# Four graph layers on one core: GpSimd waits for each pair's gathers to land in passes 3 and 4

## The chip, the core and the metric

The kernel runs on one core of one Trainium2 chip. The core has five engines that run on their own and meet at semaphores: TensorE (PE in the rows, its weight loads PEld), VectorE (DVE), ScalarE (ACT), GpSimd (POOL) and SyncE (SP). SP, ACT and POOL start transfers, and all transfers share 16 DMA engines. The metric is device time in microseconds: 3856.42 us, the median of three runs of the kernel before (3853.22 to 3861.42).

## The reference

Four message-passing layers over the same graph of 6250 nodes and 106250 edges, each added to x and followed by a layer normalisation. Cut to its core:

```python
edge_index = jnp.stack([src, dst])
x = _layernorm(x + _L0(x, edge_index, edge_attr, ...))   # MLP on [x[src], edge_attr], mean over dst
x = _layernorm(x + _L1(x, src, dst, ...))                # sum of scaled x[src], batch norm
x = _layernorm(x + _L2(x, src, dst, ...))                # mean of x[src], elu
x = _layernorm(x + _L3(x, edge_index, edge_type, edge_weight, ...))

def _rgcn_conv(x, src, dst, edge_type, edge_weight, W, root, bias):   # twice in _L3
    xj = x[src]
    m = sum over r of (edge_type == r)[:, None] * (xj @ W[r])
    m = m * edge_weight[:, None]
    return segment_sum(m, dst) + x @ root + bias
```

The edges are sorted by dst. The change is in the two convolutions of the last layer.

## The kernel before, in words

The edges are cut into 832 tiles of 128, four tiles to a group (208 groups), two groups to a pair (104 pairs). Pass 0 does layer 0, passes 1 and 2 do layers 1 and 2, and passes 3 and 4 are the two convolutions of layer 3. Each pass ends in per-node work that is woven into the pass as blocks of nodes become complete.

Passes 3 and 4 read a table in device memory, table_rel, that holds x @ W[r] for every node and each of the four relations, one row of 512 bytes each. For most pairs GpSimd fetches the eight tiles of rows: `fetch` (L649, the DMA at L652) issues one indirect DMA per tile, 128 rows of 512 bytes, by the indices in `reli`. The eight land in one of four buffers `late_gat`, and each adds 16 to that buffer's semaphore `late_gathered`. `late_pool` (L719) does so pair after pair; from the fifth pair on it waits first for `late_seg`, the count of pairs that PE has finished, since the buffer is free only then. Nothing else stands in GpSimd's queue in these passes.

ScalarE builds the weighted one-hot tiles of a pair (`late_act`, L2650; L2660 and L2665), after a wait on `late_seg` for their own four buffers. PE (`late_pe`, L1615) waits for the landed gathers, for those one-hots and for the sum's bank, and multiplies the eight tiles into the segment sum (the 16 matmuls of L1654), which raises `late_seg`. VectorE adds the sum into `acc` (L1483).

Ten pairs of a pass (h = 10, 20, ..., 100), and in pass 4 five more (h = 21, 41, ...), are not gathered: PE builds their sums as dense counts times the node matrix. That work is spread over the pairs between, in pieces: `unit_fill` and `extra_fill` (L1670, L1683; matmuls L1679, L1690), copies to SBUF by VectorE (L1489, L1582), `extra_use` and `unit_use` (L1694, L1704; L1700, L1715), and L1645 at the pair itself. In pass 3 SP stores each built piece (880 KB) in `kept`, and in pass 4 loads it again. So 94 pairs are gathered in pass 3 and 89 in pass 4, 183 in all, with 1462 gathers (one tile of padding in each pass is left out).

The wait of PE on the gathers, which the change repeats on GpSimd:

```python
pe.wait_ge(late_gathered[n % LATE], (n // LATE + 1) * 16 * PU - late_padded(n) * 16)
```

`LATE` is 4 (buffers), `PU` is 8 (tiles of a pair), n counts the gathered pairs through both passes. `gate` is a semaphore that nothing waits for.

Of the kernel before, what the change touches and what calls it, by code (L numbers as in the profile page):

```python
# [69 lines left out]
PU = 2 * U  # L70
# [8 lines left out]
LATE, LATE_HOTS, LATE_BANKS, LATE_LAG, NODE_LAG = 4, 4, 2, 2, 5  # L79
# [50 lines left out]
def gnn(nc, x_rows, x_cols, src, dst, first, etype, eweight, ea_cols, W1a, b1a, b2b, biases, weights, out):  # L130
    with ExitStack() as ctx:
# [3 lines left out]
        def sem(name):  # L135
            return ctx.enter_context(nc.semaphore(name))

        def sems(name, n):
            return [sem(f"{name}{i}") for i in range(n)]
# [199 lines left out]
        gate = sem("gate")  # L339
# [16 lines left out]
        late_gathered = sems("late_gathered", LATE)  # L356
# [292 lines left out]
        def fetch(pool, p, g, into, landed, skipped=0):  # L649
            for u in range(U - skipped):  # L650
                t = g * U + u
                pool.indirect_dma_start(into[:, u, :], None, tables[p],  # L652
                                        bass.IndirectOffsetOnAxis(ap=idx_of(p)[:, t:t + 1].bitcast(U32), axis=0)
                                        ).then_inc(landed, 16)
# [27 lines left out]
        def padded(g):  # L682
            return PADDED if g == GROUPS - 1 else 0


        def slow_pool(pool, p, before):
            if p == 3:
                pool.wait_ge(s_sources, 2)
                pool.sem_inc(gate, 1)
            def stored():  # L690
                for s, n in zip(table_stored[p], STORED[p]):
                    pool.wait_ge(s, n)
                    pool.sem_inc(gate, 1)

            with pool.If(before > 0):
                stored()
                with pool.Fori(0, before) as r:
                    for g in range(GROUPS):
                        pool.wait_ge(slow_seg, (before * (p - 1) + r) * GROUPS + (g + 1))
                        pool.sem_inc(gate, 1)  # L700
                        fetch(pool, p, g, gat[g % RING], gathered[g % RING])
            pool.wait_ge(slow_seg, before * (p * GROUPS) + RING)
            pool.sem_inc(gate, 1)
            stored()
# [14 lines left out]
        def late_pool(pool, p, before):  # L719
            slow_pool(pool, p, before)  # L720
            for i, h in enumerate(L_PAIRS[p - 3]):
                n = (p - 3) * len(G_PAIRS) + i
                if n >= LATE:
                    pool.wait_ge(late_seg, seg_of(n - LATE))
                    pool.sem_inc(gate, 1)
                for o in range(2):
                    fetch(pool, p, 2 * h + o, late_gat[n % LATE][:, o * U:(o + 1) * U, :], late_gathered[n % LATE],
                          padded(2 * h + o))


        def late_padded(n):
            lasts = (len(G_PAIRS) - 1, len(G_PAIRS) + len(L_PAIRS[1]) - 1)
            return sum(PADDED for m in lasts if m <= n and m % LATE == n % LATE)

        def seg_of(n):
            p = int(n >= len(G_PAIRS))
            return p * PAIRS + L_PAIRS[p][n - p * len(G_PAIRS)] + 1
# [2074 lines left out]
        @block.gpsimd  # L2812
        def _(pool):
            start_pool(pool)
            before = load_rounds(pool)
            pass0_pool(pool, before)
            node0_pool(pool)
            for p in (1, 2):
                wide_pool(pool, p, before)
            for p in (3, 4):  # L2820
                late_pool(pool, p, before)
# [84 lines left out]
```

## Time and profile before

| what | value |
|---|---|
| median of three runs | 3856.42 us |
| span of the profiled execution | 4761.8 us |
| PE busy | 3833.3 us (81%) |
| POOL busy | 2652.2 us (56%) |
| DVE busy | 2287.6 us (48%) |
| ACT busy | 2017.5 us (42%) |
| gathers of passes 3 and 4 (L652, table_rel) | 1462, 1385.7 us busy |
| DMA queue of GpSimd (q0) | 235.32 MB, 18.7% of 16 engines |

Only the span is given for the profiled execution; it is 905.4 us longer than the median of the runs. Shares are of the span. POOL counts as busy while it makes the descriptors of a gather; the transfer itself comes after that. "issue" is time in which an engine waited for nothing that the profile shows, and "remote" or "another core or an unknown queue" is a wait whose releaser it cannot name.

### The profile page before, as it was taken

The numbers are of one execution on the slowest core, as the hardware profiler recorded it, in microseconds if no ns is written. First come the engines' busy times: TensorE is split into PE (matmuls) and PEld (weight loads), VectorE is DVE, ScalarE is ACT, GpSimd is POOL, SyncE is SP. The second block draws the span as 40 slices with busy tenths as digits, with TensorE's granted clock in tenths as the row PEclk, the third lists the DMA queues.
The fourth block names the chain that finished last, engine by engine and source line by source line (L and its number), as shares of the span: only waits on it lengthen the run. The fifth ranks groups of instructions, "written<-read, shape, count | busy, mean of one in ns | idle before, by whom it ended". The sixth has DMA issues, their size and how long they took to land.

```text
span 4761.8 us, 69331 instructions
## 1 busy us (share of the span) xinstructions
PE 3833.3 (81%) x23096; PEld 3228.5 (68%) x23096; DVE 2287.6 (48%) x7830; ACT 2017.5 (42%) x4824; POOL 2652.2 (56%) x2744
## 2 busy tenths in 40 slices
PE   5888888888888997899577778777766777777777
PEld 4777777777776886788466666555555666766666
DVE  5777777777676555666434334333321222222222
ACT  3444434444445554565444444444443333433332
POOL 5666666566542654555565565555656556564554
PEclk7999998998899998999788888888887788888878
DMA  6555555555555664666234333333333334443333
GB/s 197 151 147 149 152 149 150 148 148 149 144 151 145 149 152 105 160 172 165 89 127 137 128 134 131 125 116 127 127 114 105 118 113 124 128 125 112 121 115 97
DMA packets 438618, 642.39 MB, mean 135 GB/s; under 512 B 266274, under 2 KB 310818, under 8 KB 438115
## 3 DMA queue, kind: packets, MB, share of 16 engines
q1 hardware_dynamic: 310162, 375.66, 25.2%
q0 software_dynamic: 100880, 235.32, 18.7%
q10 hardware_dynamic: 27202, 26.78, 1.8%
q8 instruction: 191, 3.13, 0.3%
q14 instruction: 183, 1.50, 0.1%
HBM read 468.80 MB, written 168.73 MB: 134 GB/s over the span
## 4 chain that ended last, share of the span: by engine, by line
PE 28%; another core or an unknown queue 10%; issue 8%; DVE 5%; ACT 1%; DVEq 0%; DMA 0%; POOL 0%; ACTq 0%; POOLq 0%; SPq 0%
PE bank L1715 9%; PE bank L1654 6%; PE bank L1679 4%; PE bank L1700 3%; PE bank L1690 3%; PE bank L1645 1%; DVE w_both L1489 1%; DVE work L1557 1%; DVE work L1489 1%; DVE late_lo L1537 1%; PE bank L2353 0%; PE bank L2370 0%; DVE work L1582 0%; ACT work L2665 0%
## 5 line engine op out<-in xcount | busy, mean ns | idle before, releaser
L652 POOL DMA_INDIRECT work<-table_rel,reli x1462 | 1385.7, 948 | 1060.0 <-issue 426.4
L652 POOL DMA_INDIRECT work<-table_pre,srci x831 | 816.7, 983 | 537.6 <-issue 237.3
L2660 ACT ACTIVATE work<-iota,local 128x72 f32<-128x72 f32 x1464 | 378.4, 344 | 609.1 <-remote 346.8
L1034 ACT ACTIVATE X<-bank 128x468 uint8<-128x468 f32 (+1 forms) x624 | 323.9, 545 | 708.7 <-PE bank L976 375.1
L1654 PE MATMUL bank<-work 128*128 128x72 f32 x2928 | 425.0, 290 | 245.9 <-issue 234.8
L1654 PEld LDWEIGHTS bank<-work 128*128 128x128 f32 x2928 | 417.4, 212 | 265.5 <-issue 242.5
L2665 ACT ACTIVATE work<-work,ew,src_both 128x72 f32<-128x72 f32 x1464 | 515.4, 436 | 15.7 <-remote 9.7
L937 PE MATMUL bank<-w_both,work 128*128 128x256 f32 x1664 | 473.2, 409 | 33.3 <-issue 14.5
L1406 PE MATMUL bank<-counts,piece_hi 128*128 128x468 f32 x1176 | 464.7, 395 | 28.4 <-issue 12.9
L1406 PE MATMUL bank<-counts,piece_lo 128*128 128x468 f32 x1176 | 450.2, 383 | 0.0
L949 PE MATMUL bank<-work 128*128 128x64 f32 x3328 | 423.0, 281 | 22.3 <-issue 21.4
L949 PEld LDWEIGHTS bank<-work 128*128 128x128 f32 x3328 | 417.6, 201 | 29.5 <-issue 25.0
L976 PE MATMUL bank<-X 128*128 128x234 bf16 (+3 forms) x2080 | 293.6, 269 | 158.9 <-ACT X L1034 107.9
L1582 DVE COPY work<-bank 128x440 f32<-128x440 f32 x200 | 118.5, 614 | 560.6 <-remote 307.4
L937 PEld LDWEIGHTS bank<-w_both,work 128*128 128x128 f32 x1664 | 310.8, 205 | 71.5 <-issue 31.3
L871 DVE TENSOR_TENSOR work<-work,bank 128x512 f32<-128x512 f32 x416 | 274.0, 682 | 169.5 <-PE bank L937 99.5
L976 PEld LDWEIGHTS bank<-X 128*128 128x128 bf16 x2080 | 184.4, 104 | 244.8 <-issue 169.9
L1679 PE MATMUL bank<-work,late_lo 128*128 128x440 bf16 x1050 | 260.1, 382 | 109.8 <-DVE work L1489 36.7
L825 DVE TENSOR_SCALAR X<-X 128x600 bf16<-128x600 f16 (+1 forms) x624 | 234.5, 439 | 230.8 <-PE bank L976 176.5
L652 POOL DMA_INDIRECT work<-table_mean,srci x207 | 208.7, 1008 | 175.8 <-PE bank L1392 88.5
L1489 DVE COPY w_both<-bank 128x440 f32<-128x440 f32 x200 | 118.2, 613 | 349.8 <-remote 223.4
L652 POOL DMA_INDIRECT work<-table_gcn,srci x207 | 206.5, 998 | 139.7 <-issue 63.5
(326 smaller groups left out, 6489.9 us busy)
## 6 DMA issues: line engine op xcount, KB each, us to landing
work<-ea_cols SPq DMA_DIRECT2D x208, 256.0 KB
kept<-work SPq DMA_DIRECT2D x50, 880.0 KB
kept<-w_both SPq DMA_DIRECT2D x50, 880.0 KB
work<-kept SPq DMA_DIRECT2D x50, 880.0 KB
w_both<-kept SPq DMA_DIRECT2D x50, 880.0 KB
adj<-X SPq DMA_DIRECT2D x156, 225.0 KB
work<-adj SPq DMA_DIRECT2D x60, 585.0 KB
work<-table_rel,reli POOLq DMA_INDIRECT x1462
```

The source lines that it names most:

```text
L652: pool.indirect_dma_start(into[:, u, :], None, tables[p], bass.IndirectOffsetOnAxis(ap=idx_of(p)[:, t:t + 1].bitcast(U32), axis=0)).then_i ...
L871: dve.tensor_tensor(g, g, bank[q % 2 * 2 + h][:, :], ALU.add).then_inc(pre_added, 1)
L937: mm = pe.matmul(bank[q % 2 * 2 + h][:, j * HID:(j + 1) * HID], ea[:, slot, u * P:(u + 1) * P], w1a[:, 1, :], start=True, stop=True)
L949: pe.matmul(into[:, c * WIN:(c + 1) * WIN], gat0[:, q % SLOTS0, u, c * F:(c + 1) * F], hot0[:, hq, u, 0:WIN], start=(u == 0), stop=(u == U ...
L976: mm = pe.matmul(into[:, :, A_OFF[u]:A_OFF[u] + w], hot_lo[q % HOTS][:, u, :], code[:, j % A_CODES, at:at + (hi - lo) * w].rearrange("p (h ...
L1034: act.activation(stage[:, j % A_STAGES, lo * AW:hi * AW], bank[A_BANKS_AT[b % 2]][:, 0:(hi - lo) * AW], ACT.Copy).then_inc(a_taken, 1)
L1406: mm = pe.matmul(bank[D_BANKS[step % 2]][:, 0:D * AW], x[:, i * CT + t, :], counts[n % 2][:, t, :], start=(i * CT + t == BLANK and x is pi ...
L1654: mm = pe.matmul(bank[4 + m % LATE_BANKS][:, 0:PAIR_WIN], late_gat[n % LATE][:, u, :], late_hot[:, n % LATE_HOTS, u * PAIR_WIN:(u + 1) * P ...
L1679: mm = pe.matmul(bank[A_BANKS_AT[u % 2]][:, 0:RHI * CW], late_lo[:, n // RANGES % 2, u * PIECES + i, :], late_code[n % 2 * U + u], start=( ...
L1715: mm = pe.matmul(bank[D_BANK][:, 0:U * CW].rearrange("p (u c) -> p u c", u=U), rows[:, at, :], late_a[n % 2][:, :, t, :], start=(at == BLA ...
L2660: ins = act.activation(hot3[:, u, :], iota[:, 0:PAIR_WIN], ACT.Abs, bias=local[:, t:t + 1], scale=-1.0)
L2665: ins = act.activation(hot3[:, u, :], hot3[:, u, :], ACT.Relu, bias=ew[:, t:t + 1], scale=src_lo[:, t:t + 1])
```

## The change

Behind the gathers of each pair GpSimd waits until the semaphore of that pair's buffer shows that all of them have landed, and raises `gate` by one. The count is written as a function of the pair's number.

```diff
                 for o in range(2):
                     fetch(pool, p, 2 * h + o, late_gat[n % LATE][:, o * U:(o + 1) * U, :], late_gathered[n % LATE],
                           padded(2 * h + o))
+                pool.wait_ge(late_gathered[n % LATE], late_landed(n, PU - padded(2 * h + 1)))
+                pool.sem_inc(gate, 1)
+
+        def late_landed(n, tiles):
+            before = late_padded(n - LATE) if n >= LATE else 0
+            return (n // LATE * PU + tiles - before) * 16
```

On POOL at the start of pass 3 there stood, in the kernel before (a row's waits are those that stand ahead of its first instruction):

```order
L702 ISA
L652 DMA work<-table_rel,reli 128x128 [waits slow_seg,table3_stored0,table3_stored1]
L652 DMA work<-table_rel,reli 128x128 x31
L652 DMA work<-table_rel,reli 128x128 [waits late_seg]
L652 DMA work<-table_rel,reli 128x128 x7
L652 DMA work<-table_rel,reli 128x128 [waits late_seg]
```

And at the same place in the changed kernel, with the four buffers' semaphores told apart by their numbers:

```order
L702 ISA
L652 DMA work<-table_rel,reli 128x128 [waits slow_seg,table3_stored0,table3_stored1]
L652 DMA work<-table_rel,reli 128x128 x7
L652 DMA work<-table_rel,reli 128x128 [waits late_gathered0]
L652 DMA work<-table_rel,reli 128x128 x7
L652 DMA work<-table_rel,reli 128x128 [waits late_gathered1]
L652 DMA work<-table_rel,reli 128x128 x7
L652 DMA work<-table_rel,reli 128x128 [waits late_gathered2]
L652 DMA work<-table_rel,reli 128x128 x7
L652 DMA work<-table_rel,reli 128x128 [waits late_gathered3,late_seg]
```

No gather changes its place; the first 32, which stood in one run, now stand in four, and each later pair has a second wait ahead of it. The other engines' orders are the same.

## Rows read from the trace of the kernel before

**Rows 1.** Busy time by stage: window, its length, engines (instructions), granted clock, DMA, GB/s.
```profile
core 0: us, PE busy (x) PEld busy (x) DVE busy (x) ACT busy (x) POOL busy (x), PEclk, DMA share, GB/s
0.00:1440.00 1440.00, 1203.36 (x8698) 1035.16 (x8699) 1012.28 (x4051) 585.70 (x1130) 836.93 (x857) 0.92 0.54 154
1440.00:1810.00 370.00, 346.18 (x1816) 297.27 (x1814) 210.58 (x582) 191.11 (x266) 181.15 (x183) 0.98 0.60 144
1810.00:1890.00 80.00, 67.89 (x346) 58.45 (x344) 43.24 (x117) 38.07 (x49) 34.19 (x35) 0.88 0.44 107
1890.00:2290.00 400.00, 365.15 (x1825) 308.29 (x1825) 254.67 (x721) 232.17 (x260) 214.24 (x208) 0.95 0.59 155
2290.00:2335.00 45.00, 21.45 (x79) 10.60 (x77) 29.77 (x104) 28.08 (x74) 15.00 (x16) 0.77 0.26 90
2335.00:3517.00 1182.00, 897.34 (x4999) 707.62 (x4999) 434.53 (x1253) 496.21 (x1583) 697.43 (x736) 0.84 0.38 127
3517.00:3560.00 43.00, 24.18 (x106) 18.69 (x107) 10.61 (x40) 26.09 (x80) 11.38 (x13) 0.69 0.25 85
3560.00:4762.00 1202.00, 907.77 (x5236) 792.46 (x5235) 291.95 (x966) 420.03 (x1385) 661.93 (x699) 0.81 0.38 115
```

**Rows 2.** Chain of waits by line: 2320 to 3535 us, then 3535 to 4762 us.
```profile
by line: another core or an unknown queue 25.5%; PE bank L1679 16.2%; PE bank L1715 13.8%; issue 13.4%; PE bank L1654 8.4%; DVE w_both L1489 3.1%; DVE work L1557 2.9%; DVE work L1489 2.7%; DVE late_lo L1537 2.5%; PE bank L1645 1.7%; PE bank
...
by line: PE bank L1715 22.7%; issue 18.6%; PE bank L1654 13.3%; PE bank L1700 13.1%; another core or an unknown queue 12.4%; PE bank L1690 11.3%; PE bank L1645 2.1%; DVE work L1582 1.3%; PE bank L2757 0.6%; DVE late_lo L1546 0.6%; DVE work 
```

**Rows 3.** Chain in order of time, from 3573 us: start, length, what.
```profile
3573.72 0.28 PE bank L1654
3574.00 2.52 issue
3576.52 0.28 PE bank L1654
```

**Rows 4.** Groups of instructions on POOL: line, count | busy, mean ns | idle before, releasers.
```profile
L652 POOL DMA_INDIRECT work<-table_rel,reli x1462 | 1385.7, 948 | 1060.0 <-issue 426.4 <-PE bank L1654 359.0 <-remote 215.7
```

**Rows 5.** Instructions in order of time, 4107 to 4114 us: start, length, engine, [idle before].
```profile
4107.97 1.90 PE L1654 MATMUL bank<-work 128*128 128x72 f32 x16
...
4108.94 0.95 POOL L652 DMA_INDIRECT work<-table_rel,reli  x1 [0.30 <-issue]
4110.19 0.95 POOL L652 DMA_INDIRECT work<-table_rel,reli  x1 [0.31 <-issue]
...
4112.80 2.07 ACT L2660 ACTIVATE work<-iota,local 128x72 f32<-128x72 f32 x8 [7.19 <-remote]
...
4113.55 0.94 POOL L652 DMA_INDIRECT work<-table_rel,reli  x1 [2.40 <-remote]
```

**Rows 6.** Busy time in half microseconds behind a gather that ends at 3827.47 us.
```profile
3827.50:3828.00 0.50, 0.00 (x0) 0.00 (x0) 0.00 (x0) 0.00 (x0) 0.00 (x0) 0.50 0.00 0
3828.00:3828.50 0.50, 0.00 (x0) 0.00 (x0) 0.00 (x0) 0.00 (x0) 0.00 (x0) 0.50 0.51 123
3828.50:3829.00 0.50, 0.00 (x0) 0.00 (x0) 0.00 (x0) 0.00 (x0) 0.00 (x0) 0.50 0.03 8
```

**Rows 7.** That gather in order of time, and the wait beyond it.
```profile
3826.53 0.94 POOL L652 DMA_INDIRECT work<-table_rel,reli  x1 [0.30 <-issue]
3829.81 0.34 DVE L1588 COPY w_both<-bank 128x176 f32<-128x176 f32 x1 [18.26 <-remote]
```

**Rows 8.** Chain in order of time at the start of pass 4.
```profile
3540.67 3.39 DMA table_rel<-work
3544.20 0.77 issue
3544.96 0.95 POOL work L652
...
3553.73 3.26 DMA work<-table_rel,reli
3557.03 3.69 PE bank L1654 x16
```

## The prediction

> **What bounds the kernel now.** I read the busy time by stage first [rows 1]. Pass 0 ends near 1440 us, passes 1 and 2 fill 1440 to 2290 us, and the two passes that change are the stages of 1182 and 1202 us, with a start of 45 and of 43 us ahead of them. The reader is to see that PE is nearly full in passes 1 and 2 (346 of 370 us, 365 of 400 us) and is not in passes 3 and 4 (897 of 1182 and 908 of 1202 us, at granted clocks of 0.84 and 0.81).
>
> The chain of waits says what fills the rest [rows 2]. In pass 3, 25.5% of 1215 us (310 us) is a wait whose releaser the profile cannot name and 13.4% (163 us) is "issue", in which the engine waited for nothing. In pass 4 they are 12.4% (152 us) and 18.6% (228 us) of 1227 us. Together 853 us. Looked at closely, the "issue" is odd: PE runs one matmul of 0.28 us and then stands for 2.52 us, again and again, with its operands there and no wait [rows 3]. The profiled span is 4761.8 us and the median of the runs 3856.4 us, so 905 us of this execution are not in the timed runs. Since 853 us of strange standing lie in just these two passes, I take it that most of it belongs to the profiling, and that the timed passes 3 and 4 are much shorter than 1182 and 1202 us.
>
> How short can they be? The other stages, with PE's busy time taken to the full clock, need at least 1203.36 x 0.92 = 1107 us (pass 0), 346.18 x 0.98 = 339 us and 365.15 x 0.95 = 347 us (passes 1 and 2), and with the three starts of 80, 45 and 43 us as they stand that is 1961 us [rows 1]. That leaves passes 3 and 4 at most 3856 - 1961 = 1895 us. PE's own work there at the full clock is 897.34 x 0.84 + 907.77 x 0.81 = 1489 us. GpSimd's is more: 1462 gathers with 1385.7 us busy, 0.948 us each [rows 4], and 0.30 us from the end of one to the start of the next, with nothing to wait for [rows 5], so 1385.7 + 1462 x 0.30 = 1824 us. By these rows GpSimd fills 1824 of at most 1895 us and is the bound of both passes in the timed runs. In the profiled execution it isn't: there it stands 359.0 us for L1654 and 215.7 us for unnamed releasers, because PE has not given its buffers back [rows 4].
>
> **The change, part by part.** 183 waits and as many `sem_inc` are added; nothing is removed, and no gather changes its place. Behind the wait on POOL's queue stand the next pair's eight gathers and nothing else; PE waits for those. The last wait of a pass hides under the start of pass 4 (28 us without a gather, since table_rel is still being stored) or has nothing behind it, so 181 count.
>
> The price of one wait: the time from the end of a gather's descriptors to its landing, plus the time from a semaphore to the next gather's start, less the 0.30 us that would have passed anyway. The restart is 0.77 us: the store of table_rel lands at 3544.20 and the first gather starts at 3544.96 us [rows 8]. For the landing no wait of POOL stands in the trace, so I bound it. Below: behind the gather that ends at 3827.47 us nothing else moves, 0.51 of the DMA engines' time is busy in the half microsecond to 3828.50 and 0.03 in the next [rows 6, 7], so its bytes are in between 1.03 and 1.53 us after its end. Above: the last gather of pass 4's first pair starts at 3553.73, ends its 0.95 us at 3554.68, and PE starts on it at 3557.03 us, 2.35 us later [rows 8], with two loads of 880 KB started just before. I take 1.4 us, the upper half of the quiet case, since it is quiet behind most gathers (DMA share 0.38 in both stages [rows 1]) and the semaphore comes behind the bytes.
>
> Price of one: 1.4 + 0.77 - 0.30 = 1.87 us, bounds 1.50 and 2.82 us. Of 181: 338 us, bounds 272 and 510 us. A restart that a full ring of buffers costs already isn't paid twice; I let that go, since where GpSimd is the bound its buffers are free before it comes to them.
>
> The Trainium skill ("DMA: Bandwidth & Descriptors", section "Anatomy of one DMA — SWDGE (gpsimd) path") fits about 2.0 us plus the bytes over 436 GB/s to a DMA issued from GpSimd, most of it the receipt of the last write. For 64 KB that is 2.15 us from the start, so by an estimate from that page 1.20 us behind the 0.948 us, a price of 1.67 us and a sum of 302 us; the trace, with its bytes still arriving 1.03 to 1.53 us after the end [rows 6, 7], agrees, rather on the later side.
>
> Of the 338 us some fits into what GpSimd has spare, 0 to 71 us (1895 - 1824); I take half, 35 us. After the change GpSimd needs 1824 + 338 = 2162 us for what took at most 1895, and no other engine comes near: PE 1489 us at the full clock. Sum: 3856 + 338 - 35 = 4159 us; bounds 3856 + 272 - 71 = 4057 and 3856 + 510 = 4366 us. The sum is made for the timed runs. Against the profiled span it could not be made: there the 575 us that GpSimd already stands for its buffers [rows 4] would take in all 338 us.
>
> **The rivals.**
>
> Faster, because the pauses free what the gathers hold up. At 4107.97 us PE runs a pair's 16 matmuls, done by 4109.87; ScalarE's next one-hots, which wait for that count, start at 4112.80 and GpSimd's next gather at 4113.55 us, and both only after the running gathers had ended at 4111.14 us [rows 5]. VectorE stands 18.26 us until 2.3 us after the last gather of a burst [rows 7]. So PE's increments arrive when GpSimd has gone quiet, and a pause behind every pair would let them in sooner. If that holds in timed runs too, bursts halved save half of the unnamed waits, 231 of 462 us. But GpSimd would still need its time, so this decides only where a gather costs less than in these rows: the pass must hold the added 338 us, which it does under (1895 - 338) / 1462 = 1.065 us a gather. At 0.948 us GpSimd needs 1386 + 338 = 1724 us against 1895 - 231 = 1664 us, so the gain is 1895 - 1724 = 171 us and the time 3685 us. Against it: the 0.30 us between gathers is the same in quiet and in crowded stretches, and the 853 us fit the 905 us that the timed runs do not have.
>
> Nothing, because GpSimd is not the bound in the timed runs. If the 0.30 us were the profiling's, the gathers would take 1386 us, leave 509 us, and hide all 338: 3856 us. Halfway, at 1.10 us a gather, they take 1608 us, with the waits 1946, 51 us over 1895: 3907 us.
>
> Dearer: a landing that meets the 880 KB stores and loads of `kept` more often than not, at the upper price, or PE's clock falling further as it waits more. By the upper price 4366 us.
>
> That the wait never stops GpSimd is excluded: a gather's bytes arrive over 1 us after its descriptors [rows 6], and the pair's last gather is what the wait is for.
>
> **How the numbers follow.** The forecast, 4057 to 4320 us, has a chance of 0.57. Partly hidden, 3864 to 4057 us: 0.16. Nothing, which means within 0.2% (about 8 us, what a measurement of this kernel can tell): 0.07. Faster: 0.13. Above 4320 us: 0.07. Slower is 0.57 + 0.16 + 0.07 = 0.80. The range for 8 in 10 leaves out the faster case and the dearest one, 0.20 together: 3850 to 4320 us. The likeliest time is 4159 us.
>
> **What would show it.** In the profile of the changed kernel each pair's first gather should stand 1.5 to 2.8 us, with the landing of table_rel's rows as the releaser, some 181 times, and the stands for L1654 should shrink. No burst should be longer than eight gathers, and the unnamed waits of DVE and ACT should fall below about 12 us each. The profiled span may even shrink while the timed runs grow, which would bear out that the holding belongs to the profiling. A timed run under 3864 us would say that a gather costs less than 1.065 us in timed runs, or that the increments are held there too; one near 4159 us, that GpSimd was the bound.

## The result, and the profile after

| | before | after |
|---|---|---|
| median of 4 runs in turn, us | 3855.5 (3853.22 to 3861.42) | 4358.97 (4353.01 to 4363.55) |
| ratio | | 1.1301 (1.1285 to 1.1317) |
| span of the profiled execution, us | 4761.8 in the first profile, 3861.5 in a second | 4354.7 |

The change costs 503 us, 13.0%. The forecast was 4159 us in a range of 3850 to 4320 us: the sign, the bound and the way it works were right, the time lies 200 us above the likeliest and 39 us above the range.

The profile ahead of the prediction turned out to be that of a disturbed execution (its span of 4761.8 us against a median of 3856), so a second one of the unchanged kernel was taken (before_again, below), and all of the rows after are set beside that. One run of wait_every2 below, 4983.87 us at a granted clock of 0.649 where its others had 0.92, is left out of its median. First before_again's busy time by stage, in the columns of [rows 1]; the last three rows are pass 3, the start of pass 4, and pass 4.

```profile
core 0: us, PE busy (x) PEld busy (x) DVE busy (x) ACT busy (x) POOL busy (x), PEclk, DMA share, GB/s
0.00:1965.00 1965.00, 1861.48 (x12642) 1635.54 (x12642) 1510.39 (x5454) 1068.63 (x1699) 1277.37 (x1280) 0.98 0.63 175
...
2000.00:2915.00 915.00, 820.85 (x5005) 664.28 (x5006) 442.00 (x1289) 506.41 (x1615) 692.41 (x731) 0.94 0.49 165
2915.00:2960.00 45.00, 29.61 (x127) 21.94 (x126) 10.48 (x40) 16.86 (x52) 20.37 (x22) 0.69 0.28 86
2960.00:3861.00 901.00, 804.45 (x5248) 745.10 (x5248) 291.95 (x966) 432.29 (x1427) 671.87 (x710) 0.91 0.49 155
```

The same view of the changed kernel:

```profile
0.00:1965.00 1965.00, 1862.83 (x12636) 1635.21 (x12637) 1508.86 (x5448) 1068.91 (x1697) 1273.51 (x1279) 0.98 0.63 175
...
2000.00:3160.00 1160.00, 930.79 (x5000) 732.89 (x5000) 444.38 (x1297) 508.44 (x1621) 688.16 (x728) 0.85 0.39 130
3160.00:3200.00 40.00, 25.92 (x113) 21.48 (x113) 2.99 (x14) 7.99 (x23) 21.71 (x23) 0.63 0.20 53
3200.00:4355.00 1155.00, 891.59 (x5267) 821.92 (x5266) 297.35 (x992) 441.18 (x1454) 672.29 (x711) 0.83 0.40 123
```

Passes 0 to 2 agree to a few microseconds: the first gather of pass 3 starts at 1998.24 us before and at 1999.87 us after. All of the 493 us between the two profiled executions lies in passes 3 and 4: 245 us in the one, 254 us in the other, and 5 us less in the start between. GpSimd's busy time is the same in both and fills only three fifths of its stage after, where it filled three quarters before. PE is busy for longer at a lower granted clock (0.85 for 0.94, 0.83 for 0.91); brought to the full clock it works 1531 us after and 1504 us before, so it has no more to do, it is only held back.

The chain of waits by line, from 2000 us to the end, first before_again, then the changed kernel, says by whom:

```profile
by line: POOL work L652 64.7%; issue 21.4%; DMA work<-table_rel,reli 4.9%; PE bank L1654 3.8%; PE bank L1715 1.8%; PE bank L1700 1.0%; PE bank L1690 0.5%; PE bank L1645 0.5%; PE bank L1679 0.3%; DMA table_rel<-work 0.2%; PE bank L2353 0.1%;
```

```profile
by line: POOL work L652 50.5%; issue 23.6%; DMA work<-table_rel,reli 22.9%; PE bank L1660 0.8%; PE bank L1721 0.4%; PE bank L1685 0.4%; PE bank L1651 0.2%; PE bank L2376 0.1%; PE bank L2359 0.1%; DMA table_rel<-work 0.1%; POOLq L730 0.1%; P
```

Already before, 86% of the end is set by GpSimd's gathers and the "issue" between them; the unnamed releasers of [rows 2] are gone without any change of the kernel. After, the landing of gathers takes 22.9% of 2354 us, 539 us, where it had 4.9% of 1861 us, 91 us. (L1654 has become L1660, and other lines behind the change have moved by six.)

GpSimd's gathers as a group, the answer to [rows 4], in before_again and then after (line, count, busy and mean ns, idle before and its releasers):

```profile
L652 POOL DMA_INDIRECT work<-table_rel,reli x1462 | 1386.1, 948 | 494.6 <-issue 439.1 <-DMA table_rel<-work 49.4 <-PE bank L1654 6.1
```

```profile
L652 POOL DMA_INDIRECT work<-table_rel,reli x1462 | 1382.3, 945 | 989.7 <-DMA work<-table_rel,reli 509.5
```

A gather costs the same 0.945 to 0.948 us. The idle time before gathers doubles, by 495.1 us, and that is the whole of the loss. The waits of POOL after 2000 us split it (us in total, times, longest):

```profile
POOL work L652 <- DMA work<-table_rel,reli: 509.5, 176, 6.3
POOL work L652 <- issue: 422.3, 1281, 5.4
POOL work L652 <- DMA table_rel<-work: 48.0, 2, 30.5
POOL work L652 <- PE bank L1651: 9.9, 3, 3.9
```

The 176 stands for a landing have a mean of 2.89 us. Instruction by instruction, five more are put down to something else: two among "issue" (5.38 and 3.97 us) and the three for L1651. With them it is 181 stands, as the prediction counted, 528.8 us in all, 2.92 us each. A gap of 0.30 us would have been there anyway: 181 x 2.62 = 474 us. Beyond that, 16 of the "issue" gaps are longer than 0.30 us, by 23 us together (see the last section). 474 + 23, less 4 us of busy time, are the 493 us between the two executions. The stands differ: 107 of the 181 last 2.3 to 2.6 us, 74 are longer, 20 of these over 4 us.

One stand in order of time (start, length, engine, [idle before]), with no large transfer beside it:

```profile
2071.55 0.95 POOL L652 DMA_INDIRECT work<-table_rel,reli  x1 [0.30 <-issue]
2074.10 1.24 PE L1660 MATMUL bank<-work 128*128 128x72 f32 x7 [3.77 <-DMA work<-table_rel,reli]
2074.93 0.94 POOL L652 DMA_INDIRECT work<-table_rel,reli  x1 [2.43 <-DMA work<-table_rel,reli]
```

and the chain through it (start, length, what):

```profile
2071.55 2.51 DMA work<-table_rel,reli
2074.06 0.02 issue
2074.08 0.02 POOLq L730
2074.10 0.08 issue
2074.18 0.02 POOLq L725
2074.19 0.73 issue
2074.93 0.94 POOL work L652
```

The gather's landing is told at 2074.06 us, 1.56 us after its 0.95 us; the new wait (L730) and the old one for the buffer (L725) pass through the sequencer, and the next gather starts 0.87 us after the landing. Where SP has put a store of 880 KB on its way meanwhile, the same stand looks like this:

```profile
2262.46 0.94 POOL L652 DMA_INDIRECT work<-table_rel,reli  x1 [0.30 <-issue]
...
2262.81 0.32 SPq L2422 DMA_DIRECT2D kept<-work  x1
...
2268.85 3.33 PE L1660 MATMUL bank<-work 128*128 128x72 f32 x16 [2.68 <-DMA work<-table_rel,reli]
2269.68 0.94 POOL L652 DMA_INDIRECT work<-table_rel,reli  x1 [6.28 <-DMA work<-table_rel,reli]
```

The landing now comes 6.35 us after the gather's start (2268.81), not 2.51. PE stands 2.68 us for the same landing.

### The profile page after: what moved, and what is told of

It is laid out like the page before. It is cut to its first block, busy times and chain, and to the rows that moved or that the text cites. A ratio compares the mean times of both kernels' runs of the same rounds, so it can differ in the third digit from the quotient of the medians.

```text
span 4354.7 us, 69514 instructions
## 1 busy us (share of the span) xinstructions
PE 3732.0 (86%) x23096; PEld 3223.4 (74%) x23096; DVE 2276.1 (52%) x7830; ACT 2043.7 (47%) x4824; POOL 2658.9 (61%) x2744
## 4 chain that ended last, share of the span: by engine, by line
POOL 27%; issue 13%; DMA 13%; PE 1%; ACT 0%; POOLq 0%; DVE 0%; ACTq 0%; DVEq 0%; SPq 0%
POOL work L652 27%; DMA work<-table_rel,reli 12%; PE bank L1660 0%; PE bank L1721 0%; PE bank L1685 0%; PE bank L2359 0%; DMA table_rel<-work 0%; PE bank L1651 0%; PE bank L2376 0%; POOLq L730 0%; POOLq L725 0%; PE bank L2357 0%; DVE X L2589 0%; PE bank L2456 0%; ACT L2500 0%
## 5 line engine op out<-in xcount | busy, mean ns | idle before, releaser
L1660 PE MATMUL bank<-work 128*128 128x72 f32 x2928 | 505.7, 345 | 483.9 <-DMA work<-table_rel,reli 483.7
L1660 PEld LDWEIGHTS bank<-work 128*128 128x128 f32 x2928 | 481.1, 256 | 542.1 <-DMA work<-table_rel,reli 539.4
L943 PE MATMUL bank<-w_both,work 128*128 128x256 f32 x1664 | 432.5, 385 | 18.2 <-DVE work L877 9.4
L955 PE MATMUL bank<-work 128*128 128x64 f32 x3328 | 399.2, 273 | 5.5 <-DVE hist L824 4.8
L955 PEld LDWEIGHTS bank<-work 128*128 128x128 f32 x3328 | 393.3, 193 | 12.5 <-issue 9.4
L1047 ACT ACTIVATE work<-work 128x512 f32<-128x512 f32 x416 | 254.0, 629 | 213.2 <-DVE work L877 212.0
L943 PEld LDWEIGHTS bank<-w_both,work 128*128 128x128 f32 x1664 | 289.6, 192 | 44.2 <-issue 9.8
L1588 DVE COPY work<-bank 128x440 f32<-128x440 f32 x200 | 115.8, 614 | 388.7 <-PE bank L1696 386.2
L1495 DVE COPY work<-bank 128x440 f32<-128x440 f32 x200 | 116.7, 612 | 315.9 <-PE bank L1685 315.8
L982 PE MATMUL bank<-X 128*128 128x234 bf16 (+3 forms) x2080 | 261.4, 251 | 14.2 <-ACT X L1040 13.7
```

Of the source, the lines that this page charges most:

```text
L943: mm = pe.matmul(bank[q % 2 * 2 + h][:, j * HID:(j + 1) * HID], ea[:, slot, u * P:(u + 1) * P], w1a[:, 1, :], start=True, stop=True)
L955: pe.matmul(into[:, c * WIN:(c + 1) * WIN], gat0[:, q % SLOTS0, u, c * F:(c + 1) * F], hot0[:, hq, u, 0:WIN], start=(u == 0), stop=(u == U ...
L982: mm = pe.matmul(into[:, :, A_OFF[u]:A_OFF[u] + w], hot_lo[q % HOTS][:, u, :], code[:, j % A_CODES, at:at + (hi - lo) * w].rearrange("p (h ...
L1047: act.activation(pairs, pairs, ACT.Relu).then_inc(done, 1)
L1660: mm = pe.matmul(bank[4 + m % LATE_BANKS][:, 0:PAIR_WIN], late_gat[n % LATE][:, u, :], late_hot[:, n % LATE_HOTS, u * PAIR_WIN:(u + 1) * P ...
```

## The experiments

Eleven runs follow, the first of the kernel before itself. The question came in two parts: is it the wait itself, the landing behind it, or something that the first profile showed (increments held up)? And why 2.62 us and not 1.87? Ratios, and the differences in us, are to the kernel before as timed in turn with each: median 3854.4 us for before_again, wait_prev, wait_every2 and wait_after1, 3859.88 us for seven, after_nokept, before_nokept and six_built, 3855.81 us for wait_after2, after1_nokept and after2_nokept.

**before_again**, no edit.

> The kernel before, unchanged, for a second profile. Theory A (GpSimd's gathers bound passes 3 and 4 of the kernel before): if this execution is profiled without the 905 us that the first one had on top, passes 0 to 2 end near 1965 us as in the changed kernel, passes 3 and 4 take some 1890 us, and GpSimd stands there little but its 0.30 us between gathers (under 60 us for anything else). Theory B (GpSimd is not the bound, the engines wait for each other's counts): GpSimd stands 300 us or more for L1654. Time by both: 3856 us.

3863.34 us in the one profiled execution, span 3861.5 us. From the first gather of pass 3 (1998.24 us) to the last of pass 4 (3846.92 us) GpSimd goes from gather to gather:

```profile
2508.22 0.95 POOL L652 DMA_INDIRECT work<-table_rel,reli  x1 [0.30 <-issue]
2509.47 0.94 POOL L652 DMA_INDIRECT work<-table_rel,reli  x1 [0.30 <-issue]
2510.72 0.95 POOL L652 DMA_INDIRECT work<-table_rel,reli  x1 [0.30 <-issue]
```

Of 1462 gathers none stands for over 0.6 us but the first of each pass; the stands for L1654 are 6.1 us, not 359. So GpSimd is the bound without reserve, and the held increments of [rows 5 to 7] aren't there to be released.

**seven**: seven of a pair's eight tiles are gathered, with no wait; PE waits for as many.

```diff
-                          padded(2 * h + o))
+                          o)
...
-                    pe.wait_ge(late_gathered[n % LATE], (n // LATE + 1) * 16 * PU - late_padded(n) * 16)
+                    pe.wait_ge(late_gathered[n % LATE], (n // LATE + 1) * 16 * (PU - 1))
```

> The kernel before, without any wait, but GpSimd gathers seven of a pair's eight tiles and PE multiplies what was left in the eighth place (that part of the sums is left out), so 181 gathers fewer. Theory A (GpSimd is the bound of passes 3 and 4): 181 x (0.948 + 0.305) = 227 us less, 3629 us, or some 30 us more where PE comes to be the bound in places. Theory B (GpSimd merely keeps step with PE): no change, over 3830 us.

3636.21 us, 0.9415 (0.9400 to 0.9429): 224 us (3859.88 to 3636.21) for 181 gathers fewer, which at 0.948 + 0.30 us are 226 us. Almost every microsecond taken from GpSimd comes off the end, so nearly every one put on it must be paid.

**wait_prev**: the wait stands where the change has it, but for the pair before.

```diff
+                if i:
+                    last = PU - padded(2 * L_PAIRS[p - 3][i - 1] + 1)
+                    pool.wait_ge(late_gathered[(n - 1) % LATE], late_landed(n - 1, last))
+                    pool.sem_inc(gate, 1)
```

> GpSimd waits behind each pair not for this pair's gathers but for those of the pair before, so as many waits and as many raises of gate as in the changed kernel, each for something that was issued 10 us earlier. Theory A (the price is the time to land, with nothing issued meanwhile): 3856 to 3875 us. Theory B (the waits themselves, or fewer gathers in flight, cost the time): near 4359 us, or at least half of the 503 us, over 4100.

3858.07 us, 1.0004 (0.9995 to 1.0014). Its waits of POOL:

```profile
POOL work L652 <- issue: 432.8, 1418, 0.6
...
POOL work L652 <- DMA work<-table_rel,reli: 13.4, 44, 0.3
```

The same instructions, a wait and an increment behind every pair, cost nothing: no gap grows past 0.6 us. What costs is only that the eight gathers just issued haven't landed.

**wait_every2**: the change's wait behind every second pair.

```diff
-                pool.wait_ge(late_gathered[n % LATE], late_landed(n, PU - padded(2 * h + 1)))
-                pool.sem_inc(gate, 1)
+                if i % 2:
+                    pool.wait_ge(late_gathered[n % LATE], late_landed(n, PU - padded(2 * h + 1)))
+                    pool.sem_inc(gate, 1)
```

> The wait stands behind every second pair only, for that pair's gathers. Theory A: half of the waits, half of the price: 3856 + 503 / 2 = 4108 us, between 4080 and 4130. Theory B (the buffers: a pause leaves PE without a pair in hand, which two pairs in a row would heal): under 3950 us.

4135.15 us, the median of three runs (4129.63 to 4145.44), 1.0737 (1.0706 to 1.0768): 281 us, 5 us above the range expected and somewhat more than half of the 503. POOL's view has 258.5 us in 85 stands, 3.04 us each. With the five that it puts down to something else they are 90 stands, 250 us beyond the 0.30, 2.78 us each for the 2.62 of the changed kernel. The waits add up one by one, with no slack that the first ones would use up; all 14 of the gaps of 1.86 us (last section) are there too, not half of them.

**wait_after1** and **wait_after2**: the wait for a pair stands behind the first, or the second, gather of the next.

```diff
-                for o in range(2):
-                    fetch(pool, p, 2 * h + o, late_gat[n % LATE][:, o * U:(o + 1) * U, :], late_gathered[n % LATE],
-                          padded(2 * h + o))
-                pool.wait_ge(late_gathered[n % LATE], late_landed(n, PU - padded(2 * h + 1)))
-                pool.sem_inc(gate, 1)
+                for u in range(PU - padded(2 * h + 1)):
+                    if u == 1 and i:    # wait_after2: u == 2
+                        last = PU - padded(2 * L_PAIRS[p - 3][i - 1] + 1)
+                        pool.wait_ge(late_gathered[(n - 1) % LATE], late_landed(n - 1, last))
+                        pool.sem_inc(gate, 1)
+                    t = h * PU + u
+                    pool.indirect_dma_start(late_gat[n % LATE][:, u, :], None, tables[p],
+                                            bass.IndirectOffsetOnAxis(ap=idx_of(p)[:, t:t + 1].bitcast(U32), axis=0)
+                                            ).then_inc(late_gathered[n % LATE], 16)
```

> The same wait for a pair's gathers, but put behind the first gather of the next pair, so 1.25 us of issuing lie beside the landing. In the changed kernel GpSimd stood 509.5 us in 176 waits, 2.90 us each, of which 0.30 would have passed anyway. Theory A: each wait gets 1.25 us cheaper, 2.60 - 1.25 = 1.35 us, 181 x 1.35 = 244 us more than the kernel before: 4100 us, between 4070 and 4130. Theory B (a fixed price for each wait): still near 4359 us.

> The wait behind the second gather of the next pair, so 2.50 us of issuing lie beside the landing, with the 880 KB transfers as they are. Theory A: the quiet waits (2.43 us) cost nothing more and only those beside transfers do; in the last such kernel 60 stood 3.64 us, here 3.64 - 1.25 - 0.30 = 2.1 us each, 125 us: 3980 us. Theory C (the transfers' delay is a fixed span, which the second gather hides too): 55 x (3.95 - 2.50 - 0.30) = 63 us, 3920 us or less.

wait_after1: 4197.35 us, 1.088 (1.0858 to 1.0903), 343 us lost where I had expected 244. wait_after2: 3957.79 us, 1.0261 (1.0242 to 1.0280), 102 us, between the 125 of theory A and the 63 of theory C. Their waits for landings, in this order:

```profile
POOL work L732 <- DMA work<-table_rel,reli: 331.2, 165, 5.1
```

```profile
POOL work L732 <- DMA work<-table_rel,reli: 111.6, 90, 3.6
```

(In wait_after1, 18 more gaps, 70.8 us, stand under "issue".) A gather takes 1.25 us of GpSimd's time, so one issued ahead should hide 1.25 us of a stand, 181 x 1.25 = 226 us. The first hid 160 (503 to 343), the second 241.

**after_nokept** and **before_nokept**: the 880 KB stores and loads of `kept` are cut to 16 columns, in the changed kernel and in the one before.

```diff
-                    sp.dma_start(kept[k:k + 1, :, :].rearrange("o p c -> p (o c)"), late_a[k % 2].rearrange("p u t c -> p (u t c)")
+                    sp.dma_start(kept[k:k + 1, :, :].rearrange("o p c -> p (o c)")[:, 0:16], late_a[k % 2].rearrange("p u t c -> p (u t c)")[:, 0:16]
...
-                sp.dma_start(late_a[k % 2].rearrange("p u t c -> p (u t c)"), kept[k:k + 1, :, :].rearrange("o p c -> p (o c)")
+                sp.dma_start(late_a[k % 2].rearrange("p u t c -> p (u t c)")[:, 0:16], kept[k:k + 1, :, :].rearrange("o p c -> p (o c)")[:, 0:16]
```

> The changed kernel, but SP stores and loads only 16 of the 1760 columns of each built piece, so that the 200 transfers of 880 KB are gone from passes 3 and 4 (the rest of the pieces is left as it stood, that part of the sums is wrong). Theory A1 (the landing takes longer where these transfers run beside it): the quiet stand of 2.43 us remains, 181 x (2.43 - 0.30) = 385 us over the kernel before, 4240 us. Theory A2 (the stand is a fixed latency, the long ones have another cause): 4340 to 4365 us.

> The kernel before with the same transfers cut to 16 of 1760 columns. Theory A (GpSimd's issuing bounds it): within 10 us of 3856 us. Theory B (DMA traffic bounds it): at least 50 us less.

after_nokept: 4274.8 us, 1.1066 (1.1049 to 1.1082), 415 us over before. before_nokept: 3859.38 us, 0.9997 (0.9988 to 1.0006), so without the waits these transfers cost nothing. The stands of after_nokept:

```profile
POOL work L652 <- DMA work<-table_rel,reli: 433.9, 175, 4.0
```

2.48 us each for 2.89, and 13 of the 181 longer than 2.6 us for 74: the transfers explain some 88 of the 503 us (503 less 415). The rest is the bare landing and restart, 181 x 2.18 = 394 us, and 22 us in the 14 gaps of 1.86 us of the last section; the 385 us expected had neither these gaps nor a quiet stand above 2.43 us.

**after1_nokept** and **after2_nokept**: wait_after1 and wait_after2 with the same cut of `kept` (the edits are those two together).

> The wait behind the first gather of the next pair, with the 880 KB transfers of the built pieces cut to 16 of 1760 columns (that part of the sums is wrong). With those transfers this wait cost 343 us where 244 were expected. Theory A (the missing 99 us are the transfers beside the landing; the quiet stand of 2.43 us gets 1.25 us shorter): 181 x (2.43 - 1.25 - 0.30) = 159 us over the kernel before, 4015 us. Theory B (issuing one gather ahead hides less than its 1.25 us, transfers or not): 4100 us or more.

> The same wait behind the second gather with the 880 KB transfers cut to 16 of 1760 columns (that part of the sums is wrong). Theory A: nothing is left to pay, within 15 us of the kernel before. Theory B (a wait has a price of its own beside the landing): 3900 us or more.

4045.02 us, 1.0489 (1.0472 to 1.0507), and 3863.84 us, 1.0023 (1.0014 to 1.0033). Their waits, in this order:

```profile
POOL work L732 <- DMA work<-table_rel,reli: 194.7, 165, 3.3
```

```profile
POOL work L732 <- DMA work<-table_rel,reli: 15.2, 38, 1.5
```

With all of them the cost of the wait by the gathers issued between a pair's last and the wait for it, in us over before (after and wait_prev are the ends):

| gathers ahead | 0 | 1 | 2 | a whole pair |
|---|---|---|---|---|
| as it is | 503 | 343 | 102 | 4 |
| `kept` cut | 415 | 189 | 8 | not run |

Without the large transfers the first gather hides 226 us, what 181 x 1.25 us come to, and the second nearly all that is left. That the first fits to the microsecond is luck, since 14 of the stands of after1_nokept, every twelfth pair's, take 3.35 to 3.95 us where the others have a median of 1.10 (last section). These 33 us are what its 189 us lie above the 159 expected. So the price is that of a latency which runs on while GpSimd stands. With the transfers the first gather hides less and the second more; why is not settled. That the transfers are the cause of the difference is shown by the second row, how they do it isn't.

**six_built**: since GpSimd is the bound, PE builds one more pair of pass 4 (six for five), so that eight gathers go. `X_N` and `X_EVERY` are those pairs' number and distance; `extra_use` is moved ahead of the second `extra_fill`.

```diff
-X_EVERY, X_FIRST, X_N = 20, 21, 5
+X_EVERY, X_FIRST, X_N = 16, 21, 6
...
-                if p == 4 and h in X_AT:
-                    extra_fill(pe, X_AT[h], 2)
                 if p == 4 and h - 1 in X_AT:
                     extra_use(pe, X_AT[h - 1])
+                if p == 4 and h in X_AT:
+                    extra_fill(pe, X_AT[h], 2)
```

> A version meant to beat both: in pass 4 six pairs instead of five are built by PE beside the ten, one every 16 pairs instead of 20 (and PE uses a finished piece before it fills the second half of the next), so 8 gathers fewer and 10 more pieces for PE. Theory A: 8 x 1.253 = 10 us less, 3846 us, as long as PE has the room (804 of 901 us busy in pass 4). Theory B (PE is as tight as GpSimd): 3856 us or slower by up to 60 us, the 10 pieces' own time.

3850.04 us, 0.9972 (0.9961 to 0.9983), 0.3% under the kernel before: a small gain, clear of the interval, by about the 8 x 1.25 = 10 us of the gathers gone (`extra_use` moved in the same run, so the two are not told apart):

```profile
L652 POOL DMA_INDIRECT work<-table_rel,reli x1454 | 1379.0, 948 | 489.8 <-issue 435.1 <-DMA table_rel<-work 47.0 <-PE bank L1654 7.0
```

## Why the prediction was right in its sign and short in its size

**The bound: right.** The working from the stages, 1961 us for the rest and 1824 of at most 1895 us for GpSimd, was borne out: pass 3's first gather starts at 1998.24 us, and from there to the last it is 1849 us, of which 1832 are 1462 gathers with their gaps. seven shows that it holds for the end as well, with 224 us for 181 gathers.

**The 853 us of strange standing: right to leave out, wrong in the reason.** They were put down to the profiling. before_again, before_nokept and wait_prev are profiled in the same way and have none of it, so they belong to that one execution; what made them is open. The sum rested on the timed runs, so this cost nothing. The rival "faster" took its 462 us of unnamed waits from there, and falls with them.

**The count: right.** 181 stands, by their place behind each pair.

**The price of one wait: the step that failed.** 1.87 us were taken, 2.62 measured, 135 us too little over 181. Two parts of it can be told apart. The quiet price, by after_nokept, is 181 stands of 2.48 less 0.30 us, 2.18 each: 0.31 more than taken, 56 us. The one quiet stand above shows where: the landing comes 1.56 us after the gather where I took 1.4, and the restart is 0.87 us for 0.77. The 0.77 was a misreading of [rows 8]. The store's row ends at 3540.67 + 3.39 = 3544.06 us, not at 3544.20; between lie the two waits that GpSimd's sequencer had to pass there too:

```profile
3544.06 0.02 issue
3544.08 0.02 POOLq L693
3544.10 0.08 issue
3544.18 0.02 POOLq L725
3544.20 0.77 issue
```

From the landing to the next gather it was 0.90 us already, 0.13 us or 24 us over all more than taken. The other 0.44 us of the price, 79 us over all, are the 880 KB transfers beside the landing. I had them in the rows [rows 8], as the upper bound, and set them aside since the DMA share of 0.38 [rows 1] looked quiet behind most gathers. A mean share does not tell that: the 74 stands over 2.6 us were 1.15 us longer on average than the quiet 2.43, the longest 3.85 us, and that moved the mean. The upper bound of 2.82 us did hold the measured 2.62.

The estimate from the Trainium skill ("DMA: Bandwidth & Descriptors", section "Anatomy of one DMA — SWDGE (gpsimd) path"), 2.15 us from a gather's start and a sum of 302 us, is further off: the landing measured 2.51 us from the start in the quiet stand and 6.35 us beside a store. The page's fit is for one DMA, and no run here shows one without seven others just ahead of it.

**The 35 us of slack: wrong.** GpSimd had none to spare. The 71 us between 1824 and 1895 lie where no gather can: in before_again the first one starts 37 us later than the 1961 us, pass 4 starts 18 us after the last gather of pass 3, and 13 us follow the end of the last one, 68 us together. Taking the lower end, nothing, would have followed from the prediction's own sentence that GpSimd fills the passes.

**A term that was missing:** 23 us of longer gaps behind waits (below). In sum, with 4 us less busy time: 4159 + 135 + 35 + 23 - 4 = 4348 us, against 4359 measured. Of the 11 us left, 10 are what the difference of the two profiled executions falls short of that of the medians (493 for 503).

**The range: cut below its own bound.** The bounds gave up to 4366 us, and the range ended at 4320 by leaving the top 7% out. No row excluded the upper price, so nothing spoke for stopping short of it.

**The rivals.** "Nothing, GpSimd isn't the bound" falls by seven and before_again. "Dearer" named the right mechanism, the transfers, and is true for 79 to 88 us, though the landing met them less often than not (74 of 181 stands over 2.6 us). "Faster" falls as told. Of the signs that were named, the landing as the releaser some 181 times came as told; the stands were 2.3 to 6.3 us long where 1.5 to 2.8 had been said. The lost stands for L1654 and unnamed waits and the shorter profiled span came too, but before_again has them without the change, so they tell nothing of it.

## What to carry to other kernels

A wait of an engine for the transfers that it has just issued cost here the full way from descriptors to landing plus a restart, every time, since that engine was the bound: 2.2 us in quiet and 2.6 us on average where large transfers ran in the same passes, while the same wait two gathers later costs a fifth of it or nothing. Price such a landing from rows where other queues move, since those stands that meet a transfer raise the mean. And compare the profiled execution with the median of the runs before reading anything else: where they differ by a fifth, take the bound from sums of busy time and counts, and look for a second profile.

## What the runs showed of the hardware that was not expected

The gaps of 1.86 us. In the changed kernel, in after_nokept and in wait_every2, 14 times in the two passes, the second gather after a stand starts 1.86 us after the end of the first, with nothing that the profile names:

```profile
2176.02 0.94 POOL L652 DMA_INDIRECT work<-table_rel,reli  x1 [2.51 <-DMA work<-table_rel,reli]
2178.82 0.94 POOL L652 DMA_INDIRECT work<-table_rel,reli  x1 [1.86 <-issue]
2180.06 0.94 POOL L652 DMA_INDIRECT work<-table_rel,reli  x1 [0.30 <-issue]
```

They go by count, not by time: the gathered pairs 15, 27, 39 and on to 183, every twelfth, but for pair 99, the fifth of pass 4, where a gap of about 1.03 us stands one gather later. The first profile of the kernel before has 12 of the 14 at the same pairs, with no wait for a landing in the kernel, behind stands for something else (at the two without the gap, pairs 39 and 111, GpSimd had not stood):

```profile
2484.14 0.95 POOL L652 DMA_INDIRECT work<-table_rel,reli  x1 [5.58 <-PE bank L1654]
2486.94 0.94 POOL L652 DMA_INDIRECT work<-table_rel,reli  x1 [1.85 <-issue]
```

before_again, before_nokept and wait_prev, where GpSimd doesn't stand at the pairs at all, have none, though wait_prev has as many instructions. In after1_nokept, where the wait itself is ahead of the second gather, the stand at these pairs is longer instead, 3.35 us or more for a median of 1.10. So they come where GpSimd has stood, for whatever reason, just ahead of the first or the second gather of every twelfth pair; the cause is open.

The median gap between gathers is 0.30 us in all of the runs, so a gather of 128 rows costs 1.25 us of GpSimd. In the kernels without a wait for fresh gathers their number sets the two passes: from the first gather's start to the last's it is 1849 us for 1462, 1838 us for 1454 (six_built) and 1622 us for 1281 (seven).

PE's mean granted clock is lower in the passes with pauses (the records hold two levels, full and half): 0.94 and 0.91 where it is busy for 820 of 915 and 804 of 901 us, 0.85 and 0.83 where the same work is spread over 1160 and 1155 us, and 0.97 in seven, where it is busy for 1560 of 1630 us. Since the stands and gaps of GpSimd already account for the 493 us, no run here shows that the lower clock itself cost time.
